# SyncE fetches the rows of nine groups of edges in place of six, and reads their row numbers sixteen at a time

## The reference

```
h   = relu(layernorm(x))                             # per node
l   = h @ W_l1 (64x64 and 3 times 32x32)             # per node, the table
w   = relu(ea10 @ W_fc1 ...) @ W_fc2 ...             # per edge, 192 numbers
m   = products of w, l[src] and the edge's 4 numbers # per edge
s   = segment_sum(m, dst)                            # per node
out = x + node_vec1 * (h @ W_si + s @ W_l2)          # with fixed factors
```

## Time and profile before

| | |
|---|---|
| median of three runs | 4031.98 us |
| span of the profiled execution | 4036.8 us |
| TensorE matmul busy | 3468.5 us (86%) |
| GpSimd busy | 3034.7 us (75%) |
| VectorE busy | 2059.2 us (51%) |
| ScalarE busy | 1089.5 us (27%) |
| mean granted TensorE clock | 0.805 |
| first and last gather of line 819 start | 116.8 and 4018.5 us |

### The profile page before, as it was taken

The page is one execution under the profiler, slowest core; times in us unless marked ns, Lnnn a source line. Parts: engine busy times, 40 slices in busy tenths (PEclk is TensorE's granted clock), DMA queues, the critical chain, the costliest instruction groups (busy, mean ns, idle before and its releaser), DMA issues.

```text
span 4036.8 us, 67469 instructions
## 1 busy us (share of the span) xinstructions
PE 3468.5 (86%) x17464; PEld 2022.3 (50%) x17464; DVE 2059.2 (51%) x7424; ACT 1089.5 (27%) x2487; POOL 3034.7 (75%) x3203
## 2 busy tenths in 40 slices
PE   5788888888888888888888888888888898888888
PEld 4455445445444545555555545554455454555444
DVE  7454545455445545555455454555455554545554
ACT  5222222222222222222222222222222222222222
POOL 6777777777777777777777777777777777777776
PEclk8788878788778878787887787878788887878887
DMA  9455555555555555555555555555555555555554
GB/s 315 141 148 139 137 142 136 144 143 136 136 139 142 138 142 137 140 138 145 136 144 136 141 134 143 139 140 141 138 143 137 144 137 144 136 142 134 143 145 124
DMA packets 725181, 581.64 MB, mean 144 GB/s; under 512 B 393834, under 2 KB 648126, under 8 KB 724414
## 3 DMA queue, kind: packets, MB, share of 16 engines
q1 hardware_dynamic: 568800, 308.24, 28.3%
q0 software_dynamic: 153552, 262.31, 26.6%
q10 hardware_dynamic: 2446, 6.71, 0.4%
HBM read 421.86 MB, written 155.04 MB: 143 GB/s over the span
## 4 chain that ended last, share of the span: by engine, by line
POOL 38%; DMA 25%; issue 15%; DVE 11%; PE 11%; ACT 0%; DVEq 0%; SPq 0%; POOLq 0%; ACTq 0%
POOL R L819 37%; DMA R<-l_table,src 24%; DVE R L1028 6%; DVE R L1025 4%; PE bank L1105 3%; PE bank L639 3%; PE bank L1118 2%; PE bank L1095 2%; POOL ZD L260 1%; DMA raw_rows<-ZD 0%; PE bank L662 0%; DMA x<-in_xp 0%; DVE R L1014 0%; PE bank L682 0%; DVE st L279 0%
## 5 line engine op out<-in xcount | busy, mean ns | idle before, releaser
L819 POOL DMA_INDIRECT R<-l_table,src x3115 | 2952.8, 948 | 950.2 <-issue 772.4
L1025 DVE TENSOR_TENSOR R<-bank,R 128x256 f32<-128x256 f32 x1600 | 676.9, 423 | 1889.1 <-DMA R<-l_table,src 1288.1
L1105 PE MATMUL bank<-w,hs 100*128 100x192 f32 x6446 | 1536.0, 388 | 88.4 <-DVE R L1028 86.7
L1105 PEld LDWEIGHTS bank<-w,hs 100*128 100x128 f32 x6446 | 1285.6, 228 | 493.4 <-issue 483.4
L1118 PE MATMUL bank<-R 128*32 128x320 f32 x6448 | 740.6, 536 | 419.2 <-DVE R L1028 417.4
L1028 DVE TENSOR_TENSOR R<-bank,R 128x192 f32<-128x192 f32 x3200 | 978.0, 347 | 0.0
L931 ACT ACTIVATE E<-bank 128x320 f32<-128x320 f32 x806 | 352.7, 438 | 2177.3 <-PE bank L1118 2133.0
L1095 PE MATMUL bank<-ea,w1s 10*100 10x512 f32 x1612 | 561.4, 779 | 10.3 <-DMA ea<-in_ea_p 9.5
L925 ACT ACTIVATE hs<-bank 100x512 f32<-100x512 f32 x806 | 437.5, 594 | 393.1 <-PE bank L1095 393.1
L1118 PEld LDWEIGHTS bank<-R 128*32 128x32 f32 x6448 | 149.7, 117 | 659.8 <-issue 658.6
L639 PE MATMUL bank<-ZD 128*128 128x448 f32 x776 | 393.8, 660 | 0.0
(11 more groups left out here) (109 smaller groups left out, 829.3 us busy)
## 6 DMA issues: line engine op xcount, KB each, us to landing
s_tiles<-E SPq DMA_DIRECT2D x806, 160.0 KB
R<-l_table,src POOLq DMA_INDIRECT x3115
ea<-in_ea_p SPq DMA_DIRECT2D x403, 96.0 KB
ZD<-s_tiles SPq DMA_DIRECT2D x392, 96.0 KB, 2.5
ZD<-s_tiles SPq DMA_DIRECT2D x97, 320.0 KB
psc<-l_table SPq DMA_DIRECT2D x1536, 0.6 KB
H<-l_table SPq DMA_DIRECT2D x1536, 0.6 KB
ZD<-s_tiles SPq DMA_DIRECT2D x391, 48.0 KB, 3.1
```

Of the source, the lines that this page charges most:

```text
L819: PL.indirect_dma_start(out=Y[:, g % NB, t, :], out_offset=None, in_=T, in_offset=bass.IndirectOffsetOnAxis(ap=src[:, k:k + 1], axis=0),). ...
L1025: V.tensor_tensor(p[:, :, :, 0:64], w[:, :, 0:128].rearrange("p t (s c) -> p t s c", s=2), y[:, :, 0:64].unsqueeze(2).to_broadcast([128, n ...
L1105: m = PE.matmul(b[:, o * 192:(o + 1) * 192], hs[:, g % 4, t * 128:(t + 1) * 128], w2[:, :], start=True, stop=True, skip_group_check=True)
```

## The change

Nine quads are fetched by SyncE in place of six: 88, 163, 270, 345, 419, 526, 600, 674 and 780. Their rows are spread over 82, 75, 107, 75, 74, 107, 74, 74 and 106 turns: 6.2, 6.8, 4.8, 6.8, 6.9, 4.8, 6.9, 6.9 and 4.8 rows per turn. GpSimd leaves out 30 quads in place of 27. One load fills 16 registers in place of four, in every sixteenth row, and the registers are held over the turns until each is used; the rows of a turn need not be a multiple of four any more. One semaphore per quad takes the place of two, so both halves wait for all 512 rows.

```diff
-NROW = 6
-RB = 4
+NROW = 9
+RB = 16
...
-            s_rw = [[sem(f"s_rw{i}_{u}") for u in range(2)] for i in range(len(ROW))]
+            s_rw = [sem(f"s_rw{i}") for i in range(len(ROW))]
...
-            def rows(i, b):
-
-                if b == 0:
+            held = []
+
+            def row(i, n):
+
+                if n == 0:
...
-                c, p = divmod(i * (GE // RB) + b, 128)
-                regs = [SP.alloc_register(f"row{i}_{b}_{k}") for k in range(RB)]
-                SP.load(regs, src_row[p:p + 1, c, :])
-                for k in range(RB):
-                    t, n = divmod(b * RB + k, 128)
-                    v = bass.RuntimeValue.of_register_unchecked(regs[k]).with_bounds(min_val=0, max_val=NP - 1)
-                    SP.dma_start(lone[i % 2][n:n + 1, t, :], T[bass.ds(v, 1), :]).then_inc(s_rw[i][t // 2], 16)
-                for r in regs:
-                    SP.free_register(r)
-
-            def batches(g):
+                if n % RB == 0:
+                    c, p = divmod((i * GE + n) // RB, 128)
+                    held[:] = [SP.alloc_register(f"row{i}_{n}_{k}") for k in range(RB)]
+                    SP.load(held, src_row[p:p + 1, c, :])
+                t, p = divmod(n, 128)
+                v = bass.RuntimeValue.of_register_unchecked(held[n % RB]).with_bounds(min_val=0, max_val=NP - 1)
+                SP.dma_start(lone[i % 2][p:p + 1, t, :], T[bass.ds(v, 1), :]).then_inc(s_rw[i], 16)
+                SP.free_register(held[n % RB])
+
+            def rows_at(g):
...
-                        n = GE // RB
-                        out += [(i, b) for b in range((g - lo) * n // (hi - lo), (g + 1 - lo) * n // (hi - lo))]
-                return out
+                        for n in range((g - lo) * GE // (hi - lo), (g + 1 - lo) * GE // (hi - lo)):
+                            row(i, n)
...
-                        V.wait_ge(s_rw[row_of[g]][u], 16 * 256)
+                        V.wait_ge(s_rw[row_of[g]], 16 * GE)
```

More of the change, by code:

```diff
@@ L868, in rows @@
                         SP.wait_ge(s_p, 2 * ROW[i - 2] + 2)
-                c, p = divmod(i * (GE // RB) + b, 128)
-                regs = [SP.alloc_register(f"row{i}_{b}_{k}") for k in range(RB)]
-                SP.load(regs, src_row[p:p + 1, c, :])
-                for k in range(RB):
-                    t, n = divmod(b * RB + k, 128)
-                    v = bass.RuntimeValue.of_register_unchecked(regs[k]).with_bounds(min_val=0, max_val=NP - 1)
-                    SP.dma_start(lone[i % 2][n:n + 1, t, :], T[bass.ds(v, 1), :]).then_inc(s_rw[i][t // 2], 16)
-                for r in regs:
-                    SP.free_register(r)
-            def batches(g):
-                out = []
+                if n % RB == 0:
[7 more added lines that the diff above has]
+            def rows_at(g):
                 for i, h in enumerate(ROW):
@@ L907, in build @@
                     store_rows(j)
-                for i, b in batches(g):
-                    rows(i, b)
+                rows_at(g)
                 for c in range(NCH):
```

## The result

The changed kernel takes 4021.07 us, the median of seven runs (4016.34 to 4023.7), against 4031.98 us before: a ratio of 0.9972, 95% interval 0.9962 to 0.9983, a gain of 10.9 us. The forecast was 4016.9 us, a gain of 15.0, with a range of 4012 to 4045 us.

What follows compares the result with a forecast made beforehand. The bound was taken to be GpSimd's gathers, 1.253 us each. Leaving out 12 saves 15.0 us, with no cost for SyncE's added work: 4031.98 - 15.0 = 4016.9 us, range 4012 to 4045 us.

Steps and rivals of the forecast that it cites:

- The bound: GpSimd issues gathers back to back at 1.253 us each; 12 fewer gathers save 15.0 us.
- The price L of the load: Time of SyncE's load of 16 row numbers: taken as 0.8 us, bounds 0.56 to 3.52 us.
- The bound from the fastest load of four: SyncE's load: if the fastest load's 308 ns were all per register, 77 ns each, 16 take 1.48 us.
- The third rival: SyncE becomes the bound at 220 ns a register, L = 3.52 us: 4398 us; chance 0.02.
- SyncE's idle time in dense turns: Idle time left per turn at 6.9 rows a turn: 0.44 - 0.43 L, 0.10 us at L = 0.8.
- The cushion: Delay the engines behind GpSimd can take before it waits: about 20 us plus 5, called 25 us.
- the ring `E`: Ring with three places that lets SyncE stand some turns behind the users; 5 us added for it.
- three blocks: Dense stretches of 82 + 75, 75 + 74 and 74 + 74 turns, where SyncE's delay adds up.
- first rival: At L = 1.48 us SyncE's delay outruns the cushion; 12 of the 15.0 us are lost: 4029 us; chance 0.14.
- the head and the tail stay as they are: 116.8 us ahead of the gathers and some 17 us behind them were taken as unchanged.
- fourth rival: GpSimd's gather pitch grows with the rows: 5 us lost, 4022 us; included in the forecast's 0.69 chance.
- The signs: 3103 gathers, no idle over 0.3 us ahead; 288 loads, median 0.5 to 1.3 us; SyncE's ScalarE wait 330 to 550 us.

Runs made afterwards that it cites:

- even places: Changed kernel with its nine fetched quads at even distances (92, 178, ..., 780), 86 turns each, in place of uneven ones: 4016.76 us, ratio 0.9961.
- `ea` on ScalarE: Changed kernel with the loads of `ea`, one in every second turn, issued by ScalarE in place of SyncE: 4018.54 us, ratio 0.9967.
- 32 row numbers: Changed kernel, nine quads at uneven places, with 32 row numbers per load in place of 16: 4017.78 us, ratio 0.9966.
- Six quads with the new load: Changed kernel with six fetched quads in place of nine, keeping 16 row numbers per load: 4031.62 us, ratio 0.9999.
- the old load: Changed kernel, nine fetched quads, with four row numbers per load in place of 16: 4201.33 us, ratio 1.0423.
- second even-places run: Nine quads at even distances once more, on a chip where the kernel before took 4040.85 us: 4025.7 us, ratio 0.9961.
- ten-quad kernel: Changed kernel with ten quads at even distances and the loads of `ea` on ScalarE: 4020.2 us beside 4040.85 before, ratio 0.9948.
- the same eleven quads: Eleven quads at even distances, `ea` loads on ScalarE: 4074.15 us, ratio 1.0077; with each block's nine loads on ScalarE too: 4009.65 us, ratio 0.9943.

## Why the prediction was right, point by point

- **The bound.** Right. Wherever GpSimd has no wait over 0.3 us, its gathers follow one another at 1.250 us (1.253 in the slower of the two speeds below), with 3115 to 3095 of them, and the time falls nearly by those left out: 15.1 and 15.2 us for 12 (even places, two chips), 13.4 (`ea` on ScalarE) and 14.3 (32 row numbers) for 12, 20.65 for 16, 22.4 for 20. The shortfalls of up to 2.6 us are smaller than the step of 3.3 us between the two ends. Six quads with the new load give nothing.
- **The price L of the load.** Mis-sized. I took 0.8 us by the single register that took 726 ns; it is 1.27, just inside the 0.5 to 1.3 that I had given as a sign. What made that row long is not shown, but it was not the number of registers. The bound from the fastest load of four, 77 ns a register and 1.48 us, was the better guide. The Trainium skill, "Runtime: NRT & Kernel Launch", section "Instruction fetch mechanics", gives some 200 ns per register; 63 and 57 ns were measured here from SBUF, so its figure is three times too large in this case while its form, a price for each register, fits. The third rival, which needed a price of that size, did not come.
- **SyncE's idle time in dense turns.** The formula 0.44 - 0.43 L gives -0.12 us at 1.3 us (load and gap) in place of the +0.10 that I forecast. The window from 1703 to 2060 us bears out that no idle time is left: 1.9 us of waits in 357. The size of the deficit is worked out and not measured. This is the step that failed: "idle time of 0.10 us a turn stays". SyncE's wait for ScalarE of 367.2 us lies within the forecast 330 to 550.
- **The cushion.** Mis-sized. 149 turns of -0.12 us are 18 us of delay, and GpSimd already stood at a used-up cushion, by 0.7 us. By this estimate it is about 18 to 20 us, the part that I had worked out from the ring of six quads, and near the 19 us that the trace of before shows between a copy and the gather that may follow it. The 5 us added for the ring `E` did not show; that the block loads, which wait in the same queue and which TensorE needs in order, take them away is my reading and was not tested. With 18 us instead of 25, three blocks of the old load would lose 21 us more than the 130 expected; 184 were lost, so SyncE's delay per turn with the old load was probably underrated as well.
- **The gain given back, first rival.** It came in small: it needed L = 1.48 for 12 us, and at 1.27 GpSimd loses 1.6 and 2.8 us in waits in the two traces. The median misses the forecast by 4.2 us. Against even places on one chip the changed kernel is 2.1 us slower, within the intervals. In the profiled execution the larger part, 3.2 us, lies in the longer end, which the prediction had taken as fixed: "the head and the tail stay as they are". Whether that holds for the median too is not known.
- **What was luck.** The sum had no cost for SyncE because idle time was to stay; none stayed. That the time still came within 4.2 us is due to the cushion, which took nearly all of the delay. The prediction had said so for any L up to 1.39, but it was not the reason that it relied on.
- **The pitch, fourth rival.** Did not come: a gather takes 945 or 946 ns with six, nine, ten and eleven fetched quads, but for the two speeds below, which six and nine quads show alike.
- **The signs.** 3103 gathers, 288 loads, SyncE's wait and the growth of ScalarE's wait for `s_tiles` (33.4 to 86.7 us) came as said. "No idle time over 0.3 us" did not hold, by 0.8 us. By the prediction's own words a longer wait is the sign of a wrong mechanism. What was wrong is the idle time left on SyncE; the bound by gathers stands.

## What to carry to other kernels

Where an idle queue takes work over from the bound, count its time per turn in the densest stretch and not over the whole span: SyncE had 24% of its time free before, yet nothing was left in the dense stretches after. The engine that issues DMAs has no busy share in the page; its waits per turn are its load. When such a queue is nearly full, spread the added work evenly or move other DMAs off it before adding more: the same eleven quads gave a ratio of 1.0077 or 0.9943 depending on nine loads per block alone. Look also at what else waits in its queue in order, here the loads of a block behind single rows: that is where the delay first shows, before the bound moves.

## What the hardware showed that was not expected

GpSimd's gather comes in two speeds from one execution to the next, with the same kernel and the same instructions. The even places' two profiled executions:

```profile
L821 POOL DMA_INDIRECT R<-l_table,src x3103: 942/946/962, 116.6 to 3994.8; - x194
```

```profile
L821 POOL DMA_INDIRECT R<-l_table,src x3103: 942/949/963, 117.4 to 4004.0; - x194
```

The medians are 946 and 949 ns, and the last gather starts 9.2 us later, of which 0.8 us were there at the first. The times of single runs fit two speeds: on the chip of the second even-places run, one run of the kernel before took 4032.49 us and the other nine 4039.46 to 4044.91, and the ten-quad kernel's profiled execution there, with a median gather of 946 ns, took 4011.79 us where its other four took 4019.81 to 4021.29. Those other runs have no trace. The profile that the prediction was worked out from was one with the longer gathers, so the 4.8 us by which its span stood above the median of the runs, which the sum carried over, were no fixed distance: in the changed kernel the profiled span, 4016.8 us, stands 3.9 us below that execution's time of 4020.67. The gain of 12 gathers differs by 0.03 us between the two speeds. A difference of a few us between chips or single runs must be read with that in mind; what sets the speed was not looked for.
